# Convolution part of a two-layer image kernel: one more tap of the third channel block made by ScalarE and GpSimd, ScalarE's order around gelu changed

## The chip, the cores and the metric

The kernel runs on one core of one Trainium2 chip. The metric is the device time in microseconds (us) of one launch, the median of several runs. Short names: PE is TensorE's matmul, PEld its weight load, DVE is VectorE, ACT is ScalarE, POOL is GpSimd, SP is SyncE, which issues the DMAs.

## What is computed

Eight images of 384 channels and 64x64 pixels pass two layers. The first is a group norm and a linear attention with rotary embedding. The second, in which the change lies, is cut here to its body:

```python
t = jnp.einsum('bchw,oc->bohw', x, w_in)
tp = t.reshape(b, hid, hb, P, wb, P)
tf = jnp.fft.rfft2(tp, axes=(3, 5))
tf = tf * fft_filter[None, :, None, :, None, :]
tp = jnp.fft.irfft2(tf, s=(P, P), axes=(3, 5))
t = tp.reshape(b, hid, h, w)
t = jax.lax.conv_general_dilated(t, w_dw, window_strides=(1, 1), padding='SAME', feature_group_count=hid, dimension_numbers=('NCHW', 'OIHW', 'NCHW'))
x1, x2 = (t[:, :hid // 2], t[:, hid // 2:])
g = jax.nn.gelu(x1, approximate=False) * x2
return jnp.einsum('bchw,oc->bohw', g, w_out)
```

The layer's input is group-normed first and added to its result. P is 8: the transform works on patches of 8x8 pixels. The depthwise convolution has 3x3 = 9 taps for each channel.

## The kernel before

Images run one after the other, about 434.6 us each, in three parts: part A (queries, keys, values), part B (attention output, statistics) and the convolution part, `part_c` on each engine. An image is cut into NCH = 8 chunks of 8 pixel rows (512 pixels). The 384 channels are 3 blocks of 128, k = 0, 1, 2. All orders are written by hand: each engine has one fixed list of instructions, and they meet only at semaphores.

`part_c` runs steps c = 0 to 9 as a pipeline. In step c:

- PE makes four 128-pixel tiles of chunk c: `t_tile` (w_in, 9 matmuls), `dft_tile` (L1283), `inverse_tile` (L1290). It makes the first tap of blocks 0 and 1 of chunk c-1 (`taps`, L1317; all six first taps for the last chunk), and `out_block` 0, 1, 2 of chunk c-2 (L1302 to L1306, w_out). `out_block` waits for `s_rest`, which POOL's `gated_rest` raises, and for the residual additions of DVE that free its bank.
- ACT copies each tile out of its bank (`copy_t` L634, `copy_img` L640 into the padded image `filt_img`, which lies in `big`), computes gelu of chunk c-2 (`gelu`, L647 narrow and L649 wide), rounds the gated result (`round_gated`, L656 to L659), normalises a coming chunk (L557, L567), and makes products of chunk c-1: `product(c, q)` (L670) is tap q of block 2 times its weight, written into one of four slots of `prod`.
- POOL adds products 1 to 5 into slot 0 (`add_product`, L509), adds one block of a residual (`add_residual`, L516), takes the low parts of the gated result (`gated_rest`, L522 and L524), then adds product 5, and makes the low part of a coming chunk (`low_part`, L437).
- DVE makes the other taps (`tap(c, q, k)`, L1007), each one instruction that adds into PSUM. The first DVE tap of block 2 reads the sum in slot 0 of `prod` instead of the bank, so it waits for POOL's last addition. EARLY lists the taps of chunk c-1 done in step c, LATE those of chunk c-2. DVE also multiplies by the filter (`times_filter`, L987, four in a step), gates (L1015, L1022) and adds the output to the residual (`add_out`, L939).

Slot 0 is written anew by ACT's product 0 only after the DVE tap that reads it. ACT's gelu waits for taps (8, 2) and (8, 0). The first `taps` of PE waits for gelu wide, the second for the wide gate.

## Time and profile before

| | us |
|---|---|
| median of 3 runs (3548.68 to 3550.89) | 3549.17 |
| the profiled execution | 3545.66 |
| its span in the trace | 3543.9 |
| PE busy | 3318.6 |
| DVE busy | 2981.3 |
| POOL busy | 2042.9 |
| ACT busy | 1723.4 |

The difference of 1.8 us between the profiled time and the span lies around the program. Matmuls overlap each other in the trace, so the distance from one start to the next says more of PE than its busy time. The eight images repeat the same pattern; the rows below are all of the second image, whose convolution part runs from about 757 to 932 us, except the last of them, which is of the third.

### The profile page before, as it was taken

Reading aid. Unit: us, or ns where it says so; the run is one execution under the profiler, and the core shown is the slowest. Engines: PE = TensorE matmul, PEld = TensorE weight load, DVE = VectorE, ACT = ScalarE, POOL = GpSimd, SP = SyncE. Lnnn points to the kernel's source line nnn. Section 1 sums busy time; section 2 is a strip of 40 time slices with the busy share of each in tenths; the row PEclk is TensorE's granted clock in tenths of the full one; section 3 lists DMA queues with packets and bytes.
Section 4 is the critical chain, followed back from the end, with each engine's and each line's share of the span. In section 5 each row is a group of like instructions: output and inputs, shape, how many; then the busy total and the mean of one; then the engine's idle time right before and its main releaser. Section 6 shows DMA issues by size and latency. Waiting matters only on the chain. (4 is left out here: it accounts for less than half of the span.)

```text
span 3543.9 us, 50201 instructions
## 1 busy us (share of the span) xinstructions
PE 3318.6 (94%) x17374; PEld 2872.3 (81%) x17374; DVE 2981.3 (84%) x5231; ACT 1723.4 (49%) x3159; POOL 2042.9 (58%) x1343
## 2 busy tenths in 40 slices
PE   5999999999999999999999999998999999999998
PEld 4987779877797778977789777896779967799775
DVE  7877989779898798887989879888798887888887
ACT  2433854338443474435744257442664426644275
POOL 2555755547556475564755647456565565655665
PEclk9999999999999999999999999999999999999999
DMA  6215332143321432123332233213332133331422
GB/s 224 72 36 178 106 109 72 54 161 107 122 67 63 143 132 100 63 85 125 130 101 70 90 133 124 100 54 111 113 125 99 54 131 113 113 101 52 143 99 98
DMA packets 185341, 369.89 MB, mean 104 GB/s; under 512 B 7771, under 2 KB 8835, under 8 KB 184835
## 3 DMA queue, kind: packets, MB, share of 16 engines
q1 hardware_dynamic: 185090, 366.68, 30.3%
q8 instruction: 142, 2.33, 0.3%
q14 instruction: 109, 0.88, 0.1%
HBM read 265.99 MB, written 100.66 MB: 103 GB/s over the span
## 5 line engine op out<-in xcount | busy, mean ns | idle before, releaser
L1136 PE MATMUL bank<-w_hi,x_hi 128*128 128x384 f32 x2304 | 803.5, 349 | 17.9 <-ACT vt L578 10.7
L444 POOL TENSOR_TENSOR t<-t 128x768 f32<-128x768 f32 x256 | 535.3, 2091 | 466.4 <-DVE t L841 462.4
L1137 PE MATMUL bank<-w_lo,x_hi 128*128 128x384 f32 x2304 | 781.7, 339 | 0.0
L1007 DVE SCALAR_TENSOR_TENSOR bank<-big,wdw,bank 128x512 f32<-128x512 f32 x1072 | 749.1, 746 | 20.4 <-PE bank L1317 17.3
L437 POOL TENSOR_TENSOR x_lo<-xa,x_hi 128x512 fp32r<-128x512 f32 x360 | 459.4, 1292 | 478.4 <-ACT x_hi L567 478.4
L509 POOL TENSOR_TENSOR prod<-prod 128x512 f32<-128x512 f32 x320 | 410.5, 1283 | 244.5 <-ACT prod L670 224.9
L1141 PE MATMUL bank<-w_hi,x_lo 128*128 128x384 f32 x2304 | 533.1, 339 | 0.5 <-POOL x_lo L437 0.5
L572 ACT ACTIVATE t<-t 128x384 f32<-128x384 f32 x256 | 134.7, 526 | 759.5 <-POOL t L444 747.8
L1136 PEld LDWEIGHTS bank<-w_hi,x_hi 128*128 128x128 f32 x2304 | 436.8, 190 | 23.9 <-issue 22.7
L1137 PEld LDWEIGHTS bank<-w_lo,x_hi 128*128 128x128 f32 x2304 | 437.3, 190 | 1.1
L1141 PEld LDWEIGHTS bank<-w_hi,x_lo 128*128 128x128 f32 x2304 | 415.0, 189 | 1.4 <-POOL x_lo L437 1.4
L836 DVE TENSOR_TENSOR bank<-bank,qkbias 128x384 f32<-128x384 f32 x512 | 279.6, 559 | 137.9 <-PE bank L1141 137.6
L1136 PE MATMUL bank<-win_hi,x_hi 128*128 128x384 f32 x768 | 305.4, 398 | 0.9 <-ACT x_hi L567 0.4
L670 ACT ACTIVATE prod<-big,wdw 128x512 f32<-128x512 f32 x384 | 261.5, 715 | 71.5 <-DVE bank L1007 71.2
L1290 PEld LDWEIGHTS bank<-t_mats,gb 128*128 128x128 f32 x1536 | 205.4, 191 | 89.9 <-issue 35.5
L626 ACT ACTIVATE qt_hi<-bank 128x512 fp32r<-128x512 f32 x192 | 107.4, 594 | 314.8 <-PE bank L1217 314.8
L1137 PE MATMUL bank<-win_lo,x_hi 128*128 128x384 f32 x768 | 259.9, 338 | 0.0
L841 DVE TENSOR_TENSOR t<-bank,t_csw 128x384 f32<-128x384 f32 x512 | 258.4, 545 | 0.0
L1238 PE MATMUL bank<-qt_hi,mout_hi 128*128 128x512 f32 x576 | 247.7, 430 | 0.0
L1164 PE MATMUL bank<-vt,kt 128*128 128x129 f32 x1536 | 214.8, 275 | 25.6 <-DVE kt L853 25.6
L1290 PE MATMUL bank<-t_mats,gb 128*128 128x128 f32 x1536 | 217.1, 277 | 17.8 <-ACT big L640 9.4
L1164 PEld LDWEIGHTS bank<-vt,kt 128*128 128x128 f32 x1536 | 206.9, 190 | 30.6 <-DVE kt L853 30.6
(132 smaller groups left out, 6966.8 us busy)
## 6 DMA issues: line engine op xcount, KB each, us to landing
xr<-x SPq DMA_DIRECT2D x128, 768.0 KB, 4.7
xa<-x SPq DMA_DIRECT2D x64, 768.0 KB, 6.3
x_scratch<-xr SPq DMA_DIRECT2D x64, 768.0 KB, 3.3
xa<-x_scratch SPq DMA_DIRECT2D x64, 768.0 KB, 6.0
xr<-x_scratch SPq DMA_DIRECT2D x64, 768.0 KB, 4.8
out<-xr SPq DMA_DIRECT2D x64, 768.0 KB, 3.3
big<-x SPq DMA_DIRECT2D x8, 768.0 KB, 10.2
w_raw<-wqkv_t SPq DMA_DIRECT2D x1, 1728.0 KB, 6.8
```

What stands on the lines that cost most here:

```text
L437: nc.gpsimd.tensor_tensor(dst, src, hi, ALU.subtract).then_inc(s_lo, 1)
L444: nc.gpsimd.tensor_tensor(a, a, b[:, :, ::-1, :], ALU.add).then_inc(s_add, 1)
L509: nc.gpsimd.tensor_tensor(prod[:, 0], prod[:, 0], prod[:, slot_of(q)], ALU.add).then_inc(s_padd, 1)
L670: nc.scalar.activation(prod[:, slot_of(q)].rearrange("p (r s) -> p r s", s=W), filt_img[:, 2, ds(c * ROWS + q // 3, ROWS), q % 3:q % 3 + W ...
L836: nc.vector.tensor_tensor(qk, qk, qkbias[:, b * C:(b + 1) * C], ALU.add).then_inc(s_bias, 1)
L841: ins = nc.vector.tensor_tensor(dst[:, p2, b].rearrange("p s (f r) -> p s f r", r=2), src, tab.unsqueeze(1).unsqueeze(3).to_broadcast(wide ...
L1007: nc.vector.scalar_tensor_tensor(dst, src, wdw[:, k, q:q + 1], so_far, ALU.mult, ALU.add)\
L1136: nc.tensor.matmul(dst, hi(k), whi(k), start=(k == 0), stop=False)
L1137: nc.tensor.matmul(dst, hi(k), wlo(k), start=False, stop=False)
L1141: ins = nc.tensor.matmul(dst, lo(k), whi(k), start=False, stop=(k == KB - 1))
L1164: ins = nc.tensor.matmul(bank[KVB][:, k * (P + 1):(k + 1) * (P + 1)], kt[:, p2, k * P:(k + 1) * P], vt[:, p2, k, :], start=(first and k == ...
L1290: ins = nc.tensor.matmul(bank[INVB][:, k * P:(k + 1) * P], gb[:, p2, k * P:(k + 1) * P], phi_t, start=True, stop=True)
```

## The change

Tap 6 of block 2 is no longer a DVE instruction. ACT makes it as product 6 (slot 3) and POOL adds it, both at the start of the next step, ahead of their work for the next chunk. The first DVE tap of block 2 is then (7, 2). ACT's `copy_t` of tile 0 moves ahead of products 0 to 2. In step 2 alone those three products move behind gelu. In step 1 a one-element gelu is put ahead of the last `copy_img`, so that the table load stands there. The lists LATE and LAST have a new order.

```diff
-POOL_TAPS = 6
+POOL_TAPS = 7
-LATE = [(6, 2), (6, 0), (7, 2), (7, 0), (8, 2), (8, 0), (6, 1), (7, 1), (8, 1)]
+LATE = [(6, 0), (7, 0), (7, 2), (8, 0), (8, 2), (6, 1), (7, 1), (8, 1)]
-LAST = [(6, 2), (6, 0), (7, 2), (7, 0), (8, 2), (8, 0), (6, 1), (7, 1), (8, 1)]
+LAST = LATE
...
                 def part_c(c, h, edge, par):
+                    if c >= 2:
+                        add_product(c - 2, 6)
                     if within(edge, 0, NCH, -1):
                         for q in range(1, 3):
                             add_product(c - 1, q)
...
-                            act.wait_ge(s_dw, dw_count(i, c - 1, (6, 2)))
+                            act.wait_ge(s_dw, dw_count(i, c - 1, (7, 2)))
...
-                    if conv:
+                    if gated:
+                        if c < NCH + 1:
+                            act.wait_ge(s_img, (i * 8 + c - 1) * 4 + 6)
+                        product(c - 2, 6)
+                    if tile:
+                        copy_t(T, 0)
+                    if conv and c != 2:
                         for q in range(3):
                             product(c - 1, q, edge == 1)
-                    if tile:
-                        copy_t(T, 0)
...
                     if gated:
                         gelu(c - 2, edge == NCH + 1)
+                    if c == 2:
+                        for q in range(3):
+                            product(c - 1, q)
...
                         copy_img(T + 2, c, 2)
+                        if c == 1:
+                            nc.scalar.activation(idle_act[:, :], counted[:, 31:32], ACT.Gelu)
                         copy_img(T + 3, c, 3)
...
                     if last:
-                        for q, k in LAST[:6]:
+                        for q, k in LAST[:5]:
...
                         dve.wait_ge(s_img, T + 2)
-                        tap(c - 2, 6, 2)
                         tap(c - 2, 6, 0)
+                        tap(c - 2, 7, 0)
+                    if gated:
                         tap(c - 2, 7, 2)
-                    if gated:
-                        tap(c - 2, 7, 0)
+                        tap(c - 2, 8, 0)
                         tap(c - 2, 8, 2)
-                        tap(c - 2, 8, 0)
                         tap(c - 2, 6, 1)
```

ACT's list in step 2, from its first `prod` instruction to the one behind gelu's copy. Before (`prod` is a product, `tb` a `copy_t`, `gel` gelu):

```order
L670 ACTIVATE prod<-big,wdw 128x512 x3
L634 ACTIVATE tb<-bank0 128x384
L647 ACT_TABLE_LOAD
L647 ACTIVATE gel<-bank5 64x512
L649 ACTIVATE gel<-bank6 128x512
L634 ACTIVATE tb<-bank1 128x384
L670 ACTIVATE prod<-big,wdw 128x512
```

And now:

```order
L673 ACTIVATE prod<-big,wdw 128x512
L637 ACTIVATE tb<-bank0 128x384
L650 ACTIVATE gel<-bank5 64x512
L652 ACTIVATE gel<-bank6 128x512
L673 ACTIVATE prod<-big,wdw 128x512 x3
L637 ACTIVATE tb<-bank1 128x384
L673 ACTIVATE prod<-big,wdw 128x512
```

The three products stand behind gelu, and `copy_t` of tile 1 behind them. The single product ahead is tap 6 of chunk 0.

POOL's list in step 3 and every later step with tiles. Before (`prod` is `add_product`, `xr` the residual, `g_half` and `g_lo` are `gated_rest`):

```order
L509 TENSOR_TENSOR prod<-prod 128x512 x2
L516 TENSOR_TENSOR xr<-xr,vt 128x512
L509 TENSOR_TENSOR prod<-prod 128x512 x2
L522 TENSOR_TENSOR g_half<-gel,g_top 128x512
L524 TENSOR_TENSOR g_lo<-gel,g_hi 128x512
```

And now:

```order
L510 TENSOR_TENSOR prod<-prod 128x512 x3
L517 TENSOR_TENSOR xr<-xr,vt 128x512
L510 TENSOR_TENSOR prod<-prod 128x512 x2
L523 TENSOR_TENSOR g_half<-gel,g_top 128x512
L525 TENSOR_TENSOR g_lo<-gel,g_hi 128x512
```

One addition, that of product 6 of chunk c-2, stands ahead of the rest.

DVE's list at the start of a steady step. Before (bank5 is the sum of block 2, bank6 of block 0, bank7 of block 1):

```order
L1007 SCALAR_TENSOR_TENSOR bank5<-big,wdw,prod 128x512
L1007 SCALAR_TENSOR_TENSOR bank6<-big,wdw,bank6 128x512
L1007 SCALAR_TENSOR_TENSOR bank5<-big,wdw,bank5 128x512
L1007 SCALAR_TENSOR_TENSOR bank6<-big,wdw,bank6 128x512
L1007 SCALAR_TENSOR_TENSOR bank5<-big,wdw,bank5 128x512
L1007 SCALAR_TENSOR_TENSOR bank6<-big,wdw,bank6 128x512
L1007 SCALAR_TENSOR_TENSOR bank7<-big,wdw,bank7 128x512
```

And now:

```order
L1019 SCALAR_TENSOR_TENSOR bank6<-big,wdw,bank6 128x512 x2
L1019 SCALAR_TENSOR_TENSOR bank5<-big,wdw,prod 128x512
L1019 SCALAR_TENSOR_TENSOR bank6<-big,wdw,bank6 128x512
L1019 SCALAR_TENSOR_TENSOR bank5<-big,wdw,bank5 128x512
L1019 SCALAR_TENSOR_TENSOR bank7<-big,wdw,bank7 128x512
```

One tap is gone, and the tap that reads `prod` is the third instead of the first.

## Rows read from the trace of the kernel before

**Rows 1.** Stretch, busy PE, PEld, DVE, ACT, POOL, clock, DMA share, GB/s: step 4

```profile
826.93:844.99 18.06, 17.66 (x88) 14.18 (x87) 17.45 (x28) 14.45 (x26) 13.73 (x11) 1.00 0.37 132
```

**Rows 2.** Timeline, PE, step 4: start, busy, operation [idle before <-releaser]

```profile
826.93 0.34 PE L1136 MATMUL bank<-win_hi,x_hi 128*128 128x384 f32 x1
...
827.98 0.68 PE L1141 MATMUL bank<-win_hi,x_lo 128*128 128x384 f32 x3
...
830.07 0.81 PE L1283 MATMUL bank<-tb,t_mats 128*128 128x384 f32 x2
...
837.13 0.81 PE L1283 MATMUL bank<-tb,t_mats 128*128 128x384 f32 x2
...
838.36 0.47 PE L1302 MATMUL bank<-g_hi,wout_hi 128*128 128x512 f32 x1
...
839.60 0.81 PE L1283 MATMUL bank<-tb,t_mats 128*128 128x384 f32 x2
...
841.42 0.47 PE L1302 MATMUL bank<-g_hi,wout_hi 128*128 128x512 f32 x1
...
844.99 0.34 PE L1136 MATMUL bank<-win_hi,x_hi 128*128 128x384 f32 x1
```

**Rows 3.** Timeline of DVE, same step

```profile
826.13 1.05 DVE L1007 SCALAR_TENSOR_TENSOR bank<-big,wdw,prod 128x512 f32<-128x512 f32 x1
...
831.04 0.55 DVE L987 TENSOR_TENSOR gb<-bank,fsel 128x384 f32<-128x384 f32 x1
...
840.60 0.68 DVE L939 TENSOR_TENSOR xr<-bank,xr 128x512 f32<-128x512 f32 x1
...
842.92 0.69 DVE L939 TENSOR_TENSOR xr<-bank,xr 128x512 f32<-128x512 f32 x1 [0.52 <-PE bank L1306]
```

**Rows 4.** Timeline of ACT, same step

```profile
827.27 1.96 ACT L670 ACTIVATE prod<-big,wdw 128x512 f32<-128x512 f32 x3 [1.30 <-DVE bank L1007]
...
829.13 0.47 ACT L634 ACTIVATE tb<-bank 128x384 f32<-128x384 f32 x1
...
843.52 0.51 ACT L640 ACTIVATE big<-bank 128x384 f32<-128x384 f32 x1 [1.24 <-PE bank L1290]
```

**Rows 5.** Timeline of POOL, same step

```profile
828.70 2.72 POOL L509 TENSOR_TENSOR prod<-prod 128x512 f32<-128x512 f32 x2 [2.07 <-ACT prod L670]
...
831.37 1.19 POOL L516 TENSOR_TENSOR xr<-xr,vt 128x512 f32<-128x512 f32 x1
...
836.41 1.28 POOL L524 TENSOR_TENSOR g_lo<-gel,g_hi 128x512 fp32r<-128x512 f32 x1
```

**Rows 6.** Timeline of ACT, POOL and PE, step 2 of the same image

```profile
795.60 0.60 ACT L649 ACTIVATE gel<-bank 128x512 f32<-128x512 f32 x1
...
801.17 1.27 POOL L524 TENSOR_TENSOR g_lo<-gel,g_hi 128x512 fp32r<-128x512 f32 x1
...
802.50 0.50 PE L1302 MATMUL bank<-g_hi,wout_hi 128*128 128x512 f32 x1
...
805.23 0.47 PE L1302 MATMUL bank<-g_hi,wout_hi 128*128 128x512 f32 x1
```

**Rows 7.** Timeline of DVE, steps 8 and 9 of the same image

```profile
899.04 1.34 DVE L1007 SCALAR_TENSOR_TENSOR bank<-big,wdw,prod 128x512 f32<-128x512 f32 x1 [0.59 <-ACT big L640]
...
912.11 0.76 DVE L1007 SCALAR_TENSOR_TENSOR bank<-big,wdw,prod 128x512 f32<-128x512 f32 x1 [4.75 <-POOL prod L509]
...
916.28 0.69 DVE L1015 TENSOR_TENSOR gel<-gel,bank 64x512 f32<-64x512 f32 x1
...
919.99 1.28 DVE L939 TENSOR_TENSOR xr<-bank,xr 128x512 f32<-128x512 f32 x2
```

**Rows 8.** Timeline of PE, behind two long idle times

```profile
920.82 0.69 PE L1302 MATMUL bank<-g_hi,wout_hi 128*128 128x512 f32 x1 [3.52 <-DVE xr L939]
...
1103.13 0.94 PE L1164 MATMUL bank<-vt,kt 128*128 128x129 f32 x6 [2.02 <-DVE kt L853]
...
1103.82 1.18 PE L1113 MATMUL bank<-w_hi,win_hi 128*128 128x512 f32 x4
```

More of the change, by code:

```diff
@@ L168, in build_program @@
         counted = sb("counted", [P, 32])
+        idle_act = sb("idle_act", [P, 1])
         ksum = sb("ksum", [P, KB])
@@ L535, in part_c @@
                     if within(edge, 0, NCH, -1):
-                        for q in range(3, POOL_TAPS - 1):
+                        for q in range(3, 5):
                             add_product(c - 1, q)
@@ L540, in part_c @@
                     if within(edge, 0, NCH, -1):
-                        add_product(c - 1, POOL_TAPS - 1)
+                        add_product(c - 1, 5)
                     if c != 1 and c < (NCH if i + 1 < images else NCH - 1):
@@ L1044, in part_c @@
                     if last:
-                        for q, k in LAST[:6]:
+                        for q, k in LAST[:5]:
                             tap(c - 2, q, k, last)
                         gate_narrow(c - 2, last)
-                        for q, k in LAST[6:]:
+                        for q, k in LAST[5:]:
                             tap(c - 2, q, k, last)
```

## Prediction

> **What bounds the kernel now.** I read the table of busy times by stretch first, then the timelines of the four engines over one step of the second image's convolution part. A full step takes 18.06 us; DVE is busy for 17.45 of it, PE for 17.66, ACT for 14.45, POOL for 13.73 [rows 1]. The reader is to see there that two engines are nearly full and that ACT and POOL seem to have room for one more operation each.
>
> The timelines tell more: the engines hang in loops. PE starts its step at 826.93 and the next at 844.99 [rows 2]. DVE waits in the step once, 0.52 us at 842.92, for PE's output block 1 [rows 3]; that block starts at 841.42, behind DVE's addition of 840.60 plus 0.68 [rows 2, 3]. POOL waits 2.07 us for the first product and works from 828.70 without a gap to the end of `g_lo` at 836.41 + 1.28 = 837.69 [rows 5]. PE's output block 0, which needs `g_lo`, starts at 838.36 [rows 2], 0.67 later. So the chain from ACT's first product over POOL to PE has a slack of 0.67 us at most in 18. The question of this change is when those products start.
>
> **DVE's part of the change.** One tap out of eight behind the first goes: (831.04 - 826.13 - 0.96) / 6 = 0.66 us from start to start, the first taking 0.96 of its 1.05 [rows 3]. Taps (6, 0) and (7, 0) now follow each other, and the second waits for the first; in step 9 two gates of 0.69 and three taps of one block in a row take 919.99 - 916.28 = 3.71 us [rows 7], (3.71 - 1.38) / 3 = 0.78 for each such tap, so 0.12 is lost again. The bare gain is about 0.54 us a step. What is late next: `times_filter` of tile 0 stands behind these taps and needs PE's `dft_tile`, which starts at 830.07, and DVE takes it up at 831.04 [rows 2, 3], 0.97 later. The matmul pair itself lasts 0.81, so of the 0.54 at most 0.97 - 0.81 = 0.16 can be used before DVE waits there for PE. That loop (PE's start of a step, `dft_tile`, DVE's step, output block 1, PE's next step) allows 17.9 us a step and no less.
>
> **When the products start now.** Before, they start at 827.27, right behind the end of the first DVE tap at 827.18 [rows 3, 4]: 0.34 us after PE's step begins. Now two things stand ahead of them.
>
> Loop 1, over `copy_t`. It waits for PE's tile 0, whose last matmuls end at 827.98 + 0.68, 1.73 us into PE's step [rows 2]; hand-over 0.05; the copy's 0.47 less the overlap of 0.10 (829.13 follows 827.27 by 1.86, while the three products last 1.96) is 0.37 [rows 4]. From the products to the end of `g_lo` it is 837.69 - 827.27 = 10.42, with nothing new inside (product 6's addition is done before) [rows 4, 5]. Then PE's output block 0 follows within 0.06, as in step 2 (801.17 + 1.27 = 802.44, then 802.50) [rows 6]. Block 0 to block 1 is 839.60 - 838.36 = 1.24, and a `dft_tile` with its `inverse_tile` 838.36 - 837.13 = 1.23 [rows 2]: 2.47, where it was 3.06. Block 1 to PE's next step is 844.99 - 841.42 = 3.57 [rows 2]. Sum 1.73 + 0.05 + 0.37 + 10.42 + 0.06 + 2.47 + 3.57 = 18.67 us.
>
> Loop 2, over product 6. Output block 1 to the last image copy 843.52 - 841.42 = 2.10, the copy 0.51 and 0.07 to be seen [rows 2, 4]; product 6 (1.96 + 2 x 0.10) / 3 = 0.72 [rows 4] and 0.08; POOL's addition 1.30 (half of 2.72 is 1.36 [rows 5]) and 0.05; so tap (7, 2) starts 4.83 behind block 1. It takes 0.76 with POOL idle, as at 912.11 [rows 7], then 0.09 to the products, 10.48 to output block 0, 2.47 to block 1. Sum 18.63.
>
> Both are longer than 18.06, and nearly equal. A steady step becomes 18.67: +0.61. There are four full steps (3 to 6): +2.4 us an image. DVE's saved time turns into a wait for POOL at tap (7, 2) of about half a microsecond.
>
> At tap (7, 2) the profile shows two prices: 1.05 us at 826.13 while POOL works on `low_part`, 0.76 at 912.11, where POOL had just ended [rows 3, 7]. I take 0.76, since POOL now has nothing to do until the products that wait for this tap; with 1.05 loop 2 is 18.93 and the time 8 us more, which the range holds. The Trainium skill (SBUF — State Buffer, Who interferes with whom) says that a DVE instruction with two SBUF inputs and a GpSimd instruction that reads SBUF shut each other out, and that others don't. By it this is the short tap, and the sum stays; were it the long one everywhere, as in most steps of before, the 8 us come on top. The two durations agree with it.
>
> **Step 2.** Here the products follow gelu. Gelu wide starts at 795.60 [rows 6]; the table load ahead of it is gone, but so is the early start of DVE's taps (copy, product 6, addition and tap (7, 2) come first), so I leave it there, give or take 0.2. The products then start at 796.1, and `g_lo` ends 10.42 later, less the residual that this step lacks (1.19, of which 0.05 overlaps [rows 5]): 805.4. Before it was 802.44. Output block 1 follows at 805.4 + 0.06 + 2.47 = 807.9 instead of 805.23 [rows 6]: +2.6 us (2.3 to 2.8). The table load moved to step 1 costs ACT some tenths before the last image copy, and is hidden by the same chain.
>
> **Steps 7 to 9.** In step 7 ACT carries one product more before it reaches the late image copies: 0 to 0.8, I take 0.4. In step 8 the chain runs over DVE's tap of 899.04, which waited 0.59 for ACT's image copy and ended at 900.38 [rows 7], 1.36 behind that copy. Now it is 0.07 + 0.72 + 0.08 + 1.30 + 0.05 + 0.76 = 2.98: +1.6. POOL's chain to the last addition is as long as before, plus one addition: +1.3. DVE waits for that chain (4.75 us at 912.11 [rows 7]). After it, DVE took 919.99 - 912.11 = 7.88 us to the output addition on which PE waits 3.52 us [rows 7, 8]. Now (6, 0) and (7, 0) are done before the wait; (7, 2), (8, 0), (8, 2) take 2.1, gelu narrow 0.8, and the rest the same 3.71: 6.6, so -1.3. Together +1.6 (0.8 to 2.2).
>
> **The sum.** 2.6 + 2.4 + 0.4 + 1.6 = 7.0 us an image, 56 us for eight. The profiled execution becomes 3545.66 + 56 = 3601.7; it stands 3.5 below the median, so the median becomes 3605.
>
> **Rivals.**
>
> *DVE is the bound and its time comes back.* Price: 0.54 us in six steps of eight images, 26 us, 3523; with the loop over `dft_tile` in force only 0.16, 8 us, 3541. For it: DVE is the fullest engine beside PE, and its single wait is short [rows 1, 3]. Against it: it needs the products no later than before, and the code puts a copy and an addition ahead of them. The Trainium skill (Perfetto Trace Analysis, Optimizing Scalar/DVE Operations) holds that with DVE saturated, handing work to Scalar or even GpSimd may make sense, and (Identifying the Most-Contended Engine) to optimize the engine of highest occupancy first. By that rule the sum would be this rival's; the slack of 0.67 behind POOL is what the busy shares don't show.
>
> *The steady steps keep their time.* If the products start within 0.67 us of where they started, only step 2 and the tail cost: (2.6 + 1.6) x 8 = 34, 3583. It decides at the start of the products behind PE's step: under 1.0 us it is this, at my 2.15 it is the forecast.
>
> *PE also loses its clock.* In step 2 PE would sit idle about 2 us for `g_lo` and 1 us for a copy. After 3.52 us of idle time its matmul took 0.69 instead of 0.47 [rows 2, 8]; ten of these are 2 us an image, 16 in all: 3621. Against it: behind 2.02 us of idle time four matmuls of 512 columns last 1.18 us in all [rows 8], the pace of output block 0's five in 1.24 [rows 2].
>
> **How the numbers follow.** Forecast 0.65 (3595 to 3615), steady steps unharmed 0.12 (3583), clock loss 0.10 (3621), DVE's time comes back 0.10 (3523 to 3544), no change 0.03. The range 3577 to 3632 leaves out the last two and a little at either end: the step-2 and tail bounds are 0.3 + 0.8 down and 0.2 + 0.6 up an image, 9 and 6 us, the long tap 8. 0.2% is 7 us, about what can be told from no change: faster 0.10, same 0.03, slower 0.87.
>
> **What would show it.** In the new trace: DVE waits for POOL at the tap that reads `prod` in steps 3 to 7; the products start about 2.1 us behind PE's step; POOL's `g_lo` ends right before PE's output block 0, and PE waits for it; steps of 18.7 us; in step 2 the block starts near 805.4 on the old scale. Wrong would be a PE without that wait, or steps of 18.0 us or less.

## The result, and the profile after

| | before | after |
|---|---|---|
| median, us | 3550.03 (4 runs, 3548.68 to 3552.57) | 3614.92 (4 runs, 3612.78 to 3617.21) |
| profiled span, us | 3543.9 | 3613.4 |
| mean granted clock | 0.98 | 0.979 |

The change costs 65 us: ratio 1.0182, 95% interval 1.0164 to 1.0200. The forecast was +56, 3605; the range 3577 to 3632 holds the time.

The page of the changed kernel, first its busy times (engine, busy us, share of the span, number of instructions), then groups of its table of costs (line, engine, operation, count | busy us, mean ns of one | idle time just before them and what ended most of it):

```profile
PE 3324.6 (92%) x17374; PEld 2882.3 (80%) x17374; DVE 2953.3 (82%) x5167; ACT 1767.0 (49%) x3231; POOL 2122.4 (59%) x1407
...
L1019 DVE SCALAR_TENSOR_TENSOR bank<-big,wdw,bank 128x512 f32<-128x512 f32 x1008 | 720.4, 750 | 65.0 <-PE bank L1328 54.4
...
L510 POOL TENSOR_TENSOR prod<-prod 128x512 f32<-128x512 f32 x384 | 494.4, 1287 | 298.7 <-ACT prod L673 276.3
```

DVE has 64 instructions and 28 us less than before, as intended: 8 taps in each of 8 images, at 0.44 us net. ACT and POOL have 44 and 80 us more. PE has the same instructions and stands still longer. These shares look better than before, and the kernel is slower; where the time went is read from the waits. The next rows are of the same place as before, a steady step of the second image (start, busy, operation, and in brackets the idle time before it with what ended it). DVE, ACT, POOL and PE of the changed kernel, one fence each:

```profile
839.23 0.76 DVE L1019 SCALAR_TENSOR_TENSOR bank<-big,wdw,prod 128x512 f32<-128x512 f32 x1 [0.47 <-POOL prod L510]
...
849.54 0.56 DVE L999 TENSOR_TENSOR gb<-bank,fsel 128x384 f32<-128x384 f32 x1 [0.16 <-PE bank L1294]
...
854.68 0.69 DVE L951 TENSOR_TENSOR xr<-bank,xr 128x512 f32<-128x512 f32 x1 [0.66 <-PE bank L1317]
```

```profile
837.10 0.72 ACT L673 ACTIVATE prod<-big,wdw 128x512 f32<-128x512 f32 x1
839.81 0.49 ACT L637 ACTIVATE tb<-bank 128x384 f32<-128x384 f32 x1 [1.99 <-PE bank L1152]
840.19 1.94 ACT L673 ACTIVATE prod<-big,wdw 128x512 f32<-128x512 f32 x3
```

```profile
837.90 1.30 POOL L510 TENSOR_TENSOR prod<-prod 128x512 f32<-128x512 f32 x1 [0.40 <-ACT prod L673]
841.60 2.72 POOL L510 TENSOR_TENSOR prod<-prod 128x512 f32<-128x512 f32 x2 [2.40 <-ACT prod L673]
...
849.33 1.30 POOL L525 TENSOR_TENSOR g_lo<-gel,g_hi 128x512 fp32r<-128x512 f32 x1
```

```profile
831.94 0.50 PE L1313 MATMUL bank<-g_hi,wout_hi 128*128 128x512 f32 x1 [0.50 <-POOL g_lo L525]
834.45 0.48 PE L1313 MATMUL bank<-g_hi,wout_hi 128*128 128x512 f32 x1
...
844.00 1.10 PE L1328 MATMUL bank<-big,tapdiag 128*128 128x512 f32 x2 [0.43 <-ACT gel L652]
850.67 0.50 PE L1313 MATMUL bank<-g_hi,wout_hi 128*128 128x512 f32 x1 [0.51 <-POOL g_lo L525]
853.17 0.48 PE L1313 MATMUL bank<-g_hi,wout_hi 128*128 128x512 f32 x1
```

Output block 0 comes every 850.67 - 831.94 = 18.73 us where it was 18.06 [rows 1, 2]. POOL had been waited for by nobody in this step; now PE waits 0.50 us for its `g_lo`. The products start at 840.19, behind a `copy_t` that waits 1.99 us for PE's tile 0. DVE's gain has become waits: 0.47 for POOL, 0.16 and 0.66 (before 0.52 [rows 3]) for PE.

Step 2 of the same image, ACT and then PE:

```profile
796.40 1.28 ACT L734 ACT_TABLE_LOAD   x1
...
802.63 0.59 ACT L650 ACTIVATE gel<-bank 64x512 f32<-64x512 f32 x1 [2.95 <-DVE bank L1019]
...
803.74 1.93 ACT L673 ACTIVATE prod<-big,wdw 128x512 f32<-128x512 f32 x3
```

```profile
803.99 1.10 PE L1328 MATMUL bank<-big,tapdiag 128*128 128x512 f32 x2 [1.03 <-ACT gel L652]
806.10 0.91 PE L1294 MATMUL bank<-tb,t_mats 128*128 128x384 f32 x2 [1.02 <-ACT tb L637]
813.21 0.50 PE L1313 MATMUL bank<-g_hi,wout_hi 128*128 128x512 f32 x1 [1.77 <-POOL g_lo L525]
```

PE waits three times, 3.82 us in all, behind an ACT that sits idle for 2.95 us. DVE's tap (7, 2), on which product 0 waits, ends at 801.22, so for the last 1.4 us of that time ACT could have made products.

To compare runs I count from one mark, ACT's root of the group norm's variance, which opens the convolution part (757.55 us in the second image before, 765.50 after). Between it and the table load for exp that follows the part, before took 171.0 us on average over the seven images that have one, after 179.0: 8.0 an image, 64 in eight. The change's cost lies here. The rest of an image, whose code is the same in all kernels of this document, takes 263.6 us on average in the profile of before, 264.3 in that of after and 264.2 to 265.1 in those of the experiments.

### The profile page after: what moved, and what is told of

It reads as the page before. It is cut to its first block and busy times, and to the rows that moved or that the text cites. A ratio compares the mean times of both kernels' runs of the same rounds, so it can differ in the third digit from the quotient of the medians.

```text
span 3613.4 us, 50449 instructions
## 1 busy us (share of the span) xinstructions
PE 3324.6 (92%) x17374; PEld 2882.3 (80%) x17374; DVE 2953.3 (82%) x5167; ACT 1767.0 (49%) x3231; POOL 2122.4 (59%) x1407
## 5 line engine op out<-in xcount | busy, mean ns | idle before, releaser
L1019 DVE SCALAR_TENSOR_TENSOR bank<-big,wdw,bank 128x512 f32<-128x512 f32 x1008 | 720.4, 750 | 65.0 <-PE bank L1328 54.4
L510 POOL TENSOR_TENSOR prod<-prod 128x512 f32<-128x512 f32 x384 | 494.4, 1287 | 298.7 <-ACT prod L673 276.3
L673 ACT ACTIVATE prod<-big,wdw 128x512 f32<-128x512 f32 x448 | 306.4, 716 | 19.9 <-DVE bank L1019 18.0
L1328 PE MATMUL bank<-big,tapdiag 128*128 128x512 f32 x416 | 205.2, 609 | 41.1 <-ACT gel L652 41.1
L999 DVE TENSOR_TENSOR gb<-bank,fsel 128x384 f32<-128x384 f32 x256 | 141.8, 554 | 115.2 <-PE bank L1294 93.6
```

Source lines behind the costliest of these rows:

```text
L510: nc.gpsimd.tensor_tensor(prod[:, 0], prod[:, 0], prod[:, slot_of(q)], ALU.add).then_inc(s_padd, 1)
L673: nc.scalar.activation(prod[:, slot_of(q)].rearrange("p (r s) -> p r s", s=W), filt_img[:, 2, ds(c * ROWS + q // 3, ROWS), q % 3:q % 3 + W ...
L1019: nc.vector.scalar_tensor_tensor(dst, src, wdw[:, k, q:q + 1], so_far, ALU.mult, ALU.add)\
```

## The experiments

"Before" is always the kernel before, timed together with that row's kernel on the same chip. "Behind the mark" is the distance from that root in the second image.

| kernel | median, us | before, us | ratio (95%) | steady step |
|---|---|---|---|---|
| the change | 3614.9 | 3550.0 | 1.0182 (1.0164 to 1.0200) | 18.73 |
| step 2 undone | 3591.5 | 3544.5 | 1.0126 (1.0108 to 1.0143) | 18.71 |
| products first | 3641.4 | 3544.5 | 1.0264 (1.0247 to 1.0281) | 19.36 |
| gated rest first | 3641.0 | 3544.5 | 1.0265 (1.0245 to 1.0286) | 19.54 |
| two sums | 3621.1 | 3544.5 | 1.0209 (1.0191 to 1.0227) | 18.72 |
| addition 6 small | 3593.3 | 3547.4 | 1.0123 (1.0110 to 1.0137) | 18.71 |
| residual small | 3592.6 | 3547.4 | 1.0123 (1.0107 to 1.0138) | 18.34 |
| gelu's load alone | 3553.5 | 3549.8 | 1.0010 (1.0001 to 1.0019) | 18.07 |
| two sums, products first | 3607.0 | 3549.8 | 1.0161 (1.0147 to 1.0175) | 18.83 |
| the same, POOL holds | 3565.3 | 3547.4 | 1.0042 (1.0029 to 1.0054) | 17.95 |
| the same, repaired | 3539.0 | 3548.4 | 0.9975 (0.9966 to 0.9984) | 17.98 |
| before, sum sooner | 3536.3 | 3548.4 | 0.9968 (0.9955 to 0.9980) | 18.06 |
| repaired, hold in the tail | 3544.1 | 3549.7 | 0.9982 (0.9973 to 0.9991) | 17.97 |

The steady step is output block 0 to output block 0, the mean of the four from step 3 to step 7; before it was 18.06.

### Step 2 undone

```diff
-                    if conv and c != 2:
+                    if conv:
                         for q in range(3):
                             product(c - 1, q, edge == 1)
...
-                    if c == 2:
-                        for q in range(3):
-                            product(c - 1, q)
```

> The changed kernel with one part undone: in step 2 the products 0 to 2 stand ahead of gelu again, as in all other steps. Theory (the chain from ACT's products over POOL's additions and gated_rest to PE's output block 0 sets the time): in the changed kernel the products of step 2 start at 803.74, behind gelu; ahead of it they can start right behind tap (7, 2), which ends at 801.22, so about 2.4 us sooner; output block 0 comes 2.4 sooner (PE itself would be ready about then), 19 us in all for eight images: 3596 us. Rival (gelu and the first taps of PE, which wait for it, are what step 2 hangs on): gelu comes 0.5 us or more later than now, so the kernel gets slower by 4 us or more, 3619.

Measured 3591.5. Output block 0 of step 2 comes 45.33 us behind the mark, where it came 47.71 after the change and 44.95 before. PE of this kernel:

```profile
805.92 1.10 PE L1325 MATMUL bank<-big,tapdiag 128*128 128x512 f32 x2 [1.70 <-ACT gel L652]
812.09 0.50 PE L1310 MATMUL bank<-g_hi,wout_hi 128*128 128x512 f32 x1
```

The wait for `g_lo` is gone and the one for gelu is longer, 1.70 instead of 1.03. By the ratios 0.0056 of 3550, 20 us, a third of the whole cost, is the special order of step 2. That order alone served gelu and delayed everything POOL does. With it undone block 0 of step 2 comes only 0.4 us later than before the change, so nearly all that is lost in this step comes from the order and not from the seventh tap.

### Two other orders of the same work

Products ahead of `copy_t` again, as before:

```diff
-                    if tile:
-                        copy_t(T, 0)
                     if conv and c != 2:
                         for q in range(3):
                             product(c - 1, q, edge == 1)
+                    if tile:
+                        copy_t(T, 0)
```

> The changed kernel with ACT's products 0 to 2 ahead of the first copy_t again, as before the change (step 2 as changed). Theory: the products gain nothing, because tap (7, 2), on which product 0 waits, ends at 839.99 and they start at 840.19 now; but the copy then stands behind them and reaches PE's first dft_tile 1.2 us late, and with it times_filter and all of DVE's step. Steady step 19.3 us instead of 18.73, five steps: 3633 to 3640 us. Rival (the copy alone delays the products): faster, steady step near 18.1, 3590.

Measured 3641.4 over a kernel before of 3544.5, so 97 us, 1 us over the expected range; the step of 19.3 came as expected. ACT and PE of a steady step:

```profile
844.79 0.72 ACT L673 ACTIVATE prod<-big,wdw 128x512 f32<-128x512 f32 x1
847.77 1.95 ACT L673 ACTIVATE prod<-big,wdw 128x512 f32<-128x512 f32 x3 [2.26 <-DVE bank L1019]
849.63 0.47 ACT L637 ACTIVATE tb<-bank 128x384 f32<-128x384 f32 x1
```

```profile
850.16 0.91 PE L1294 MATMUL bank<-tb,t_mats 128*128 128x384 f32 x2 [1.13 <-ACT tb L637]
```

Loop 2 is closed over `copy_t` here: product 6, addition 6, tap (7, 2), products, and only then the copy, for which PE waits 1.13 us. The step is 19.36. So the change's move of `copy_t` is a repair that its seventh tap needs; it holds the loss in a steady step to 0.67 us where it would be 1.3.

`gated_rest` ahead of additions 3 and 4 in steps 2 to 7, so that `g_lo` comes sooner:

```diff
+                    if 2 <= c < NCH:
+                        gated_rest(c - 2)
                     if within(edge, 0, NCH, -1):
                         for q in range(3, 5):
                             add_product(c - 1, q)
-                    if c >= 2:
+                    if c >= NCH:
                         gated_rest(c - 2)
```

> The changed kernel with POOL's gated_rest moved ahead of its additions of products 3 and 4 in steps 2 to 7. Theory (PE waits for g_lo behind POOL's additions): in a steady step g_half can start when the rounding is done, 6.95 us behind the first product, and g_lo ends at about 9.56 instead of 10.45; output block 0 no longer waits, and the next loop (gelu wide, PE's first taps, the third dft_tile, times_filter, output addition) sets the step at 18.3 to 18.4 instead of 18.73; in step 2 output block 0 comes 1.6 us sooner. Per image 1.6 + 5 x 0.36 = 3.4, 27 us in all: 3588 us. Rival (tap (7, 2) and product 6 hold the step, whatever POOL's order): no change, 3615. Rival (DVE lost its time to PE through gelu alone): no change in the steady step.

Measured 3641.0: wrong, and by much. POOL, DVE and PE:

```profile
830.21 1.30 POOL L523 TENSOR_TENSOR g_half<-gel,g_top 128x512 fp32r<-128x512 f32 x1 [1.75 <-ACT gel L662]
...
832.71 4.14 POOL L510 TENSOR_TENSOR prod<-prod 128x512 f32<-128x512 f32 x3
836.81 3.78 POOL L438 TENSOR_TENSOR x_lo<-xa,x_hi 128x512 fp32r<-128x512 f32 x3
840.54 1.29 POOL L510 TENSOR_TENSOR prod<-prod 128x512 f32<-128x512 f32 x1
```

```profile
841.87 0.76 DVE L1021 SCALAR_TENSOR_TENSOR bank<-big,wdw,prod 128x512 f32<-128x512 f32 x1 [1.75 <-POOL prod L510]
```

```profile
846.53 1.10 PE L1330 MATMUL bank<-big,tapdiag 128*128 128x512 f32 x2 [1.60 <-ACT gel L654]
```

PE no longer waits for `g_lo`. But POOL now idles 1.75 us for the rounded gate, pays for it behind, and from 830.21 to 841.83 has no gap; addition 6 comes late, DVE's tap waits 1.75 for it, and gelu with PE behind it 1.60. POOL looked 59% busy over the span, yet in this order it has no room between one wait that is built in (tap to products) and the next.

### Which loop sets the step

The two loops of the prediction were 18.67 and 18.63, too near to each other for the step's length to tell them apart. Addition 6 stands in loop 2 alone:

```diff
-                    nc.gpsimd.tensor_tensor(prod[:, 0], prod[:, 0], prod[:, slot_of(q)], ALU.add).then_inc(s_padd, 1)
+                    w = 1 if q == 6 else CHUNK
+                    nc.gpsimd.tensor_tensor(prod[:, 0, :w], prod[:, 0, :w], prod[:, slot_of(q), :w], ALU.add).then_inc(s_padd, 1)
```

> The change, with POOL's seventh-tap addition cut to one column of 512 (the rest of that tap's product is left out of the result). It takes about 1.2 us out of the loop over product 6, that addition and the tap (forecast 18.63), and nothing between PE's tile 0 and g_lo (forecast 18.67). Theory A (the loop through copy_t(T,0), the products, POOL and g_lo sets the steady step): the step stays at 18.7 us; only steps 2, 8 and 9, where the addition stands on the path, get 1.2 us shorter at two or three places: 3590 to 3606 us. Rival B (POOL's total work sets the step): the step falls by 0.6 to 0.7, the whole by 2.4 per image more: 3565 to 3585 us.

Measured 3593.3, and the steady step is unchanged. POOL and PE:

```profile
836.23 0.19 POOL L511 TENSOR_TENSOR prod<-prod 128x1 f32<-128x1 f32 x1 [0.37 <-ACT prod L674]
839.94 2.72 POOL L511 TENSOR_TENSOR prod<-prod 128x512 f32<-128x512 f32 x2 [3.52 <-ACT prod L674]
```

```profile
830.28 0.50 PE L1314 MATMUL bank<-g_hi,wout_hi 128*128 128x512 f32 x1 [0.49 <-POOL g_lo L526]
...
849.00 0.50 PE L1314 MATMUL bank<-g_hi,wout_hi 128*128 128x512 f32 x1 [0.48 <-POOL g_lo L526]
```

849.00 - 830.28 = 18.72. POOL is given 1.1 us of room in each step and uses it to wait longer, 3.52 instead of 2.40. The 21 us that the kernel gains come from step 2 (0.7 us an image) and the tail. Part of the tail's gain, 0.9 us an image, lies behind PE's long wait there, where the granted clock stayed higher, and not in the addition itself. So loop 1, and not loop 2, sets the steady step.

The residual addition stands in both loops:

```diff
-                    nc.gpsimd.tensor_tensor(mine, mine, proj_c, ALU.add).then_inc(s_res, 1)
+                    nc.gpsimd.tensor_tensor(mine[:, :1, :1], mine[:, :1, :1], proj_c[:, :1, :1], ALU.add).then_inc(s_res, 1)
```

> The change, with POOL's residual addition cut to one element (the rest of that residual is left out of the result). The addition stands in both loops, so both get about 1.1 us shorter, to 17.5 us, under the 18.06 us that PE's work takes. Theory A: the steady step is 18.0 to 18.1 us again, the output block waits for PE's own order and not for g_lo, and the whole is 3590 to 3602 us (four or five steps of 0.65 us and up to 0.9 us in steps 3 to 7's neighbours, times 8 images). Rival B (the step is set by something that doesn't run through POOL): the step stays at 18.7 us and the whole within 4 us of the change, 3611 to 3619 us.

Measured 3592.6, inside what was expected, but not by the step that was expected: 18.34, not 18.0 to 18.1. ACT and PE:

```profile
836.93 0.49 ACT L637 ACTIVATE tb<-bank 128x384 f32<-128x384 f32 x1 [1.95 <-PE bank L1152]
837.32 1.94 ACT L673 ACTIVATE prod<-big,wdw 128x512 f32<-128x512 f32 x3
...
839.76 0.59 ACT L650 ACTIVATE gel<-bank 64x512 f32<-64x512 f32 x1
```

```profile
841.12 1.10 PE L1328 MATMUL bank<-big,tapdiag 128*128 128x512 f32 x2 [0.42 <-ACT gel L652]
```

The wait for `g_lo` is gone and a third loop remains, which the prediction didn't have: PE's tile 0, `copy_t`, the products and both gelus, which now run one behind the other on ACT without a gap, and PE's taps, which wait 0.42. From the copy to PE's taps it is 841.12 - 836.93 = 4.19, in the changed kernel too (844.00 - 839.81). From the taps to output block 0, to block 1 and to the next copy it is 6.16, 2.65 and 5.34 in this kernel's rows: with the 4.19 together 18.34, the step. In the changed kernel this loop is hidden under loop 1.

### Two sums

The change starts the sum of a chunk in slot 0 and must wait with product 0 until DVE has read the last one. With a sum for even and one for odd chunks that wait goes:

```diff
-                    nc.gpsimd.tensor_tensor(prod[:, 0], prod[:, 0], prod[:, slot_of(q)], ALU.add).then_inc(s_padd, 1)
+                    nc.gpsimd.tensor_tensor(prod[:, c % 2], prod[:, c % 2], prod[:, slot_of(c, q)], ALU.add).then_inc(s_padd, 1)
...
-                            act.wait_ge(s_dw, dw_count(i, c - 1, (7, 2)))
+                        if c >= 2:
+                            act.wait_ge(s_dw, dw_count(i, c - 2, (7, 2)))
```

> The changed kernel with two slots for the sum of the products, used in turn by even and odd chunks (the other products share the two remaining slots), so that product 0 no longer waits for tap (7, 2) of the chunk before; ACT's order as changed. Theory (two loops of equal length hold the products: tap (7, 2), and the first copy_t, which waits for PE's tile 0): freeing one of the two moves nothing, 3612 to 3616 us, steady step 18.7. Rival (the added hop ACT, POOL, DVE of product 6 alone is the cause): the products start at once and the step falls to 18.1, 3585 or less. Seen by now: with both holds taken away the kernel took 3607, so a time near 3615 or a little over is likelier than 3585.

Measured 3621.1, a little over what was expected; the two ratios' intervals overlap. The steady step is 18.72 as with one sum, as loop 1 says: that order never waited for the slot. The convolution part takes 179.2 us behind the mark, the change's 179.0: it loses 1.8 us in step 2 (49.54 for block 0), where only two slots are left for the other products, and gets nearly all of it back in the tail, 1.0 us by a granted clock that stayed higher behind PE's long wait.

Two sums and the products first, without the order of step 2:

```diff
                     if conv:
                         for q in range(3):
                             product(c - 1, q, edge == 1)
+                    if tile:
+                        copy_t(T, 0)
```

> The changed kernel with both holds on the products taken away at once: two slots for the sum in turn (product 0 doesn't wait for tap (7, 2) of the chunk before) and products 0 to 2 ahead of the first copy_t, in step 2 too. All the work is that of the changed kernel: seven products on ACT, six additions on POOL, eight other taps less one on DVE. Theory (it is when the products start, not how much work ACT and POOL have): the products start about 0.3 us ahead of PE's step, g_lo is early again, and the loop over PE's first dft_tile and DVE holds the step at 17.9 us; the last steps save 0.7 us. About 1.4 us an image under the kernel before: 3538 us. Rival (the added product and addition, 0.7 and 1.3 us a step, are themselves too much): 3600 or more. Rival (product 6's hop still delays DVE at tap (7, 2) and gelu with it): between the two, 3560.

Measured 3607.0, far from 3538 and in the range of the rival by which the added work is too much in itself. DVE and POOL:

```profile
838.71 1.78 DVE L1016 SCALAR_TENSOR_TENSOR bank<-big,wdw,prod 128x512 f32<-128x512 f32 x1 [0.48 <-POOL prod L510]
```

```profile
837.37 4.25 POOL L510 TENSOR_TENSOR prod<-prod 128x512 f32<-128x512 f32 x3 [0.16 <-ACT prod L673]
```

The tap that reads `prod` takes 1.78 us where it took 0.76. POOL no longer stops for it: the first of the three additions makes the sum that the tap reads, the second starts with the tap. Gelu then waits 1.60 us for DVE (in this kernel's ACT timeline), and the step is 18.83. So the wait that I had taken away was also what kept the two engines apart. If that is so, it must help to put a wait in:

```diff
                     if within(edge, 0, NCH, -1):
+                        if c >= 2:
+                            gp.wait_ge(s_dw, dw_count(i, c - 2, (7, 2)))
                         for q in range(1, 3):
                             add_product(c - 1, q)
```

> The kernel of two sums with the products first, with one more wait: POOL begins the next chunk's additions only when DVE's tap (7,2), which reads the other sum from SBUF, is done; the one-element gelu is left out. Theory A (in the run before this one that tap took 1.77 us instead of 0.76 because POOL's additions ran beside it, and gelu, the gates and PE waited for that microsecond): the tap is back at about 0.76 us, DVE gives the gelu its bank 1.0 us sooner, POOL's additions start 1.1 us later, which the 1.64 us that POOL waits ahead of the low parts takes up; the steady step goes from 18.83 to 18.0 to 18.2 us and the whole to 3540, between 3532 and 3552 us, as fast as the kernel before or a little faster. Rival B (the tap's length is its own, two operands from SBUF): it stays at 1.77 us, the additions only come later, and the whole is 3610 to 3640 us. Rival C (the tap is short, but POOL's chain of additions, residual and g_lo is then the last to arrive at the output block): step 18.4 to 18.8, the whole 3565 to 3605 us.

The one-element gelu of step 1 is left out too; alone it costs some 4 us, below. Measured 3565.3; by the ratios 42 us less, nearly all by one added wait, with the added product and addition still there. So they are not what made 3607. DVE, POOL and ACT:

```profile
850.13 0.76 DVE L1015 SCALAR_TENSOR_TENSOR bank<-big,wdw,prod 128x512 f32<-128x512 f32 x1 [0.47 <-POOL prod L509]
```

```profile
850.97 2.73 POOL L509 TENSOR_TENSOR prod<-prod 128x512 f32<-128x512 f32 x2 [0.87 <-DVE bank L1015]
```

```profile
788.82 0.72 ACT L674 ACTIVATE prod<-big,wdw 128x512 f32<-128x512 f32 x1 [2.05 <-POOL prod L509]
...
798.02 1.28 ACT L651 ACT_TABLE_LOAD   x1 [1.06 <-DVE bank L1015]
```

The tap is 0.76 again and the step 17.95, 0.1 shorter than before the change. That is the mechanism shown, from both sides. The 14 traces of this case hold 896 such taps: 675 ran with POOL idle and took 0.75 or 0.76 us each; 221 began while a POOL instruction was under way and took 0.84 to 1.78, and every one of these ended 0.55 to 0.56 us after that instruction did, whichever it was. POOL pays too: in the kernel of 3607 the addition that begins during the tap takes 1.53 to 1.56 us instead of 1.29.

The Trainium skill (SBUF — State Buffer, Who interferes with whom) states it: a DVE instruction with two SBUF inputs contends for a shared read interface with a GpSimd instruction that reads SBUF, the lock is exclusive, and the order of issue decides who is blocked. The traces agree with it. By that rule an addition of 1.29 us that has just begun and then the tap's own 0.76 would make about 2.0, an estimate; 1.78 is what stands here, because only 0.56 of the tap is left when POOL ends.

The total missed, 3565 instead of 3540. That is the edge of rival C's range, but the longer step by which C gets there (18.4 to 18.8) is not there. The last two rows are of steps 1 and 2: with two sums only two slots are left for the other products, so ACT waits 2.05 us in step 1, and the table load stands behind a wait of 1.06 us for DVE. Output block 0 of step 2 is 46.78 behind the mark, not 44.95.

### Gelu's table sooner, alone

The kernel before with the one-element gelu of the change in step 1:

```diff
                        copy_img(T + 2, c, 2)
+                        if c == 1:
+                            nc.scalar.activation(idle_act[:, :], counted[:, 31:32], ACT.Gelu)
```

> The kernel before with one part of the change alone: the one-element gelu in step 1, so that the table load stands there. Theory: in step 2 of before gelu narrow starts at 794.98 behind a load of 1.28; without the load gelu, product 3 and g_lo come about 1.2 us sooner, and output block 0 of step 2 with them, less 0.3 us for the image copy that the load now delays: 0.6 to 1.1 us an image, 3541 to 3545 us. Rival (the load was hidden by PE or DVE): no change, 3550.

Measured 3553.5 to 3549.8: no gain, rather 0.1% lost. DVE and ACT in step 2:

```profile
792.11 0.76 DVE L1010 SCALAR_TENSOR_TENSOR bank<-big,wdw,prod 128x512 f32<-128x512 f32 x1 [0.31 <-ACT big L641]
```

```profile
795.60 0.59 ACT L648 ACTIVATE gel<-bank 64x512 f32<-64x512 f32 x1 [0.31 <-DVE bank L1010]
```

The load delays the image copy behind it; DVE starts step 2 0.31 us late, and gelu, rid of its load, waits 0.31 for DVE. Output block 0 stands 44.85 behind the mark instead of 44.95, and the whole part takes 171.5 instead of 171.0; 0.3 of that lies behind PE's long wait of the tail, where the granted clock differs from image to image.

### A version that beats both, and its control

Three repairs on the kernel in which POOL holds: three slots for the products of chunk 0 (whose other sum is not yet in use), the table load into the 1.06 us in which ACT waits in step 2, and, in the last product step, additions 5 and 6 ahead of `gated_rest`:

```diff
-            return c % 2 if q == 0 else 3 - q % 2
+            if q == 0:
+                return c % 2
+            return 1 + (q - 1) % 3 if c == 0 else 3 - q % 2
...
+                    if c == 2:
+                        nc.scalar.activation(idle_act[:, :], counted[:, 31:32], ACT.Gelu)
                     if 3 <= c <= NCH:
...
+                    if c == NCH:
+                        for q in range(5, 7):
+                            add_product(c - 1, q)
                     if c >= 2:
                         gated_rest(c - 2)
```

> The kernel of two sums in which POOL holds its additions for the tap, with three repairs where its trace still shows time lost against the kernel before. (1) The first chunk of an image has three slots for its products instead of two: ACT's fifth product waited 2.05 us for a slot in step 1, with copy_t behind it, and the last picture copy of that step came 1.0 us late. (2) gelu's table is loaded in step 2 behind copy_t(T,0), in the 1.06 us in which ACT waits for DVE, by a one-element gelu there. (3) In the last product step POOL adds products 5 and 6 ahead of the gated rest: the last chunk's tap (7,2) waited 1.96 us for that sum, and the output block of that step had 3.7 us to spare. Theory A: steps 2 to 7 are then 0.3 us shorter than the kernel before's over all, the tail loses 1.3 to 2.0 us of its 35.34 us from the output block of step 7 to the last one (34.65 in the kernel before); in all 1.0 to 2.0 us per image faster than the kernel before: 3532 to 3541 us at 3547 us for that one. Rival B: step 2 is held by POOL (product 6, then the wait for the tap, then four additions and the rest), the repairs 1 and 2 give half, and only the tail is better: 3540 to 3552 us.

Measured 3539.0 (11 runs, 3535.0 to 3542.7): 0.25% under the kernel before. Output block 0 of step 2 is back at 44.97 behind the mark and that of step 7 at 134.69 (before 135.00, with POOL holding 136.04). From there to the first output block of the last chunk it takes 32.57 us, where it took 34.65 and 35.34. That is 2.8 less, over the 1.3 to 2.0 expected: half of it is DVE's earlier chain, half a faster PE (5.36 us instead of 6.86 for the stretch behind its long wait). That half was not planned: on average over seven images the part ends 7.4 us behind that wait instead of 8.3, because the granted clock stayed higher, some 7 us in eight images. The last section comes back to it.

The third repair has nothing to do with the seventh tap, so the kernel before got it too, with its one late addition:

```diff
+                    if c == NCH:
+                        add_product(c - 1, POOL_TAPS - 1)
                     if c >= 2:
                         gated_rest(c - 2)
```

> The kernel before with one change: in the last product step POOL adds product 5 ahead of the gated rest and not behind it. Control for repair 3 of the run beside it: how much of its gain has to do with the seventh tap. In the kernel before DVE's tap (6,2) of the last chunk waits 4.75 us for that sum, until 912.11 us; the sum would be there 2.55 us sooner, and g_lo 1.3 us later, at 912.2, where the output block starts at 914.5. Theory A: DVE's last chain starts 2.2 to 2.5 us sooner and takes add_out and the last output block with it: 3527 to 3533 us at 3547 us for the kernel before. Rival B: the last chain then waits for PE's taps of the last chunk instead, and 0 to 1 us per image is left: 3539 to 3547 us.

Measured 3536.3 (5 runs, 3532.4 to 3540.5), between the two theories. DVE of this kernel, last step:

```profile
909.12 1.75 DVE L1009 SCALAR_TENSOR_TENSOR bank<-big,wdw,prod 128x512 f32<-128x512 f32 x1 [2.65 <-POOL prod L509]
```

Before, that wait was 4.75 [rows 7]. The tap starts 2.1 us sooner, but now beside POOL's `g_half`, and takes 1.75 instead of 0.76. So 1.1 us are gained there, and the part takes 169.8 us behind the mark instead of 171.0. The intervals of this kernel and the repaired one overlap: six products for block 2 with this one line are as good as seven with all repairs. In the two traces the repaired kernel reaches the end of PE's long wait 0.3 us sooner in an image, 2 us in eight, which the times don't resolve. The whole idea of a seventh tap is worth nothing that I can measure, even carried out well.

The last run held POOL in the tail too:

```diff
                         for q in range(5, 7):
                             add_product(c - 1, q)
+                        gp.wait_ge(s_dw, dw_count(i, c - 1, (7, 2), True))
```

> The repaired kernel with POOL holding its additions for the tap once more: in the last product step the gated rest begins only when DVE's tap (7,2) of the last chunk is done. In the repaired kernel that tap took 1.54 us (910.17) beside POOL's additions and g_half (909.89); alone such a tap took 0.76 us. Theory A (the length comes from POOL's operation beside it): the tap is 0.76 us again, DVE's last chain of the image is 0.7 to 0.8 us shorter, g_half starts 0.7 us later, for which the output block has 0.4 us; 0.4 to 0.8 us per image less: 3532 to 3537 us at 3548.4 us for the kernel before. Rival B (the tap waits for something else there, PE's taps or the clock): it stays at 1.5 us and the whole at 3538 to 3542 us.

Measured 3544.1: a miss; it gains nothing, and by the ratios is rather 2 us behind (their intervals overlap). DVE and ACT of this kernel, then ACT's same row of the repaired one:

```profile
910.17 0.76 DVE L1029 SCALAR_TENSOR_TENSOR bank<-big,wdw,prod 128x512 f32<-128x512 f32 x1
```

```profile
913.54 0.59 ACT L658 ACTIVATE gel<-bank 64x512 f32<-64x512 f32 x1 [5.67 <-POOL g_lo L527]
```

```profile
913.12 0.59 ACT L657 ACTIVATE gel<-bank 64x512 f32<-64x512 f32 x1 [5.26 <-DVE bank L1028]
```

The tap is 0.76 and not 1.54, as theory A had it. But I had looked for `g_lo`'s slack only at the output block. Gelu writes into the buffer that `g_lo` reads, so the held `g_lo` holds gelu, 0.42 us later than without, and everything behind it.

## Why the prediction was right, step by step

**The direction and the mechanism** were right: the slack of POOL's chain behind PE, not DVE's busy share, decides. The rival by which DVE's time comes back fell in this order of the code. The Trainium skill (Perfetto Trace Analysis, Optimizing Scalar/DVE Operations) says that with DVE saturated, handing work to Scalar or even GpSimd may make sense. Here it didn't: DVE had 28 us less to do and the kernel took 65 us more.

**Loop 1**, forecast 18.67, is 18.73 from output block 0 to the next. Its terms in the rows of after: output block 1 to the copy 839.81 - 834.45 = 5.36 (forecast 3.57 + 1.73 + 0.05 = 5.35), copy to products 0.38 (0.37), products to the end of `g_lo` 850.63 - 840.19 = 10.44 (10.42), to block 0 0.04 (0.06), block 0 to 1 2.50 (2.47). Each is off by 0.03 at most. That it is this loop and not loop 2 the small addition 6 has shown.

**Loop 2**, forecast 18.63, was not the bound. The price of 0.76 for the tap was right, and for the reason given: POOL idles there.

**DVE's gain.** The wait of 0.47 for POOL at the tap was forecast as about half a microsecond, and DVE waits for PE ahead of `times_filter` (0.16).

**Step 2**, forecast +2.6 at output block 1 (its terms, 805.4 + 0.06 + 2.47 against 805.23, make 2.7): against the mark it is 50.21 instead of 47.68, +2.53. Gelu wide came 0.3 us sooner than where the forecast left it, and the way from the products to block 0 is 0.1 longer. Undone, it gave back 20 us, 2.5 an image.

**Steady steps 3 to 6**, forecast +2.4: block 1 of step 2 to block 1 of step 6 is 74.92 against 72.31, +2.61.

**Step 7**, forecast +0.4: block 1 of step 6 to block 2 of step 7 is 21.13 against 20.67, +0.46. **Steps 8 and 9**, forecast +1.6 up to the output addition on which PE waits: +1.64. Two rows of DVE there:

```profile
928.62 0.76 DVE L1019 SCALAR_TENSOR_TENSOR bank<-big,wdw,prod 128x512 f32<-128x512 f32 x1 [2.25 <-POOL prod L510]
...
935.18 1.28 DVE L951 TENSOR_TENSOR xr<-bank,xr 128x512 f32<-128x512 f32 x2
```

The three parts hold one by one: POOL's first addition of step 8 comes 1.55 us later behind block 2 of step 7 (forecast 1.6), from it to this tap it is 1.41 longer (1.3), and from the tap to the output addition 935.18 - 928.62 = 6.56 instead of 7.88 (6.6). Together 7.2 an image against 7.0.

**What was short** is for the most part a term that wasn't there: PE's clock behind its long wait of the tail. From the output block that ends this wait to the end of the part it is 7.75 us before and 8.22 after, on average over seven images. PE in the tail, of before in [rows 8] and of after here, then the table by stretch (stretch, then PE, PEld, DVE, ACT, POOL busy with counts, granted clock, DMA share, GB/s), one stretch of after and then one of before:

```profile
936.01 0.76 PE L1313 MATMUL bank<-g_hi,wout_hi 128*128 128x512 f32 x1 [3.77 <-DVE xr L951]
```

```profile
940.00:942.00 2.00, 2.00 (x8) 2.00 (x7) 2.00 (x5) 0.44 (x1) 2.00 (x2) 0.53 0.86 331
```

```profile
923.00:925.00 2.00, 2.00 (x10) 1.99 (x8) 1.68 (x4) 1.71 (x3) 0.40 (x1) 0.67 0.00 0
```

Before, the clock was at half behind the wait of 3.52 us [rows 8] and back some 3.5 us after its end (0.67 in this stretch, then 1.00). After, behind 3.77 us, it is at half from 936 to 938 and on to nearly 942. The part ends 8.2 and 8.3 us behind that block in these two images, so they differ little; the others make the difference. Where the clock stays at 1.00 or falls late it is 7.2 or 7.3, as in three images of before (the first, fifth and sixth) and in none of after, which has 7.8 once and 8.3 six times. The rival had PE lose its clock in step 2, in every image; it did so once in eight, in the third image, behind the wait of 1.80 us at 1257.84, where block 0 to block 1 took 3.46 us instead of 2.50. So the clock did cost about 3 us in the tail and 1 to 2 us in step 2: it was the right suspect at the wrong place.

The sum, by image: up to PE's long wait 7.2 more in five images, 7.5 in the first and 9.1 in the third, 53 in seven; 0.5 behind the wait in each of the seven, 3; and 8.5 in the last image, up to its last output block. That is 64.5, and the medians differ by 65. Why the first image has 0.3 more and the last 1.2 more than the 7.2 is not shown.

**What the prediction didn't see** is the third loop of 18.34 over gelu, and that PE waits 0.43 us in it already. It changes no number, but any repair of loop 1 ends there, as the small residual did.

## What to carry to other kernels

An engine at 59% can have no room: where the engines hand one sum round in loops, cost an added instruction at the loop that it stands in, with every buffer that its result holds, and not at the busy shares. When a wait is taken away, ask what it kept apart; POOL and a DVE instruction with two SBUF inputs were faster with a wait between them, some 40 us for one line. And test a rearrangement on the old kernel as well: the part that brought the gain here had nothing to do with the change.

## What was unexpected in the hardware

- The tap that reads `prod` and `big`, both in SBUF, has several durations for the same 128x512 work: 0.76 us with POOL idle (839.23), 1.05 to 1.34 us in places of the kernel before [rows 3, 7], up to 1.78 us with a POOL instruction that started just ahead. One rule gives them all: it ends 0.56 us after the POOL instruction that was under way at its start. The taps that read PSUM and `big` take 0.66 us from start to start beside the same POOL work. The Trainium skill's section above names this pair.
- The low clock behind PE's long wait of the tail doesn't follow the length of that wait. In one execution of the repaired kernel the wait is 2.19 to 2.24 us in each of the first seven images. Up to the first output block of the last chunk PE then took 5.36 us in three of them, with a granted clock of 1.00 throughout, 5.93 in three more and 6.45 in one, with the clock at half for a part of it. Behind 2.93 us (small residual, second image) it stayed at 1.00 too; behind 2.65 (hold in the tail) it was at 0.53 from 920 to 922, and behind 3.77 (the change) at half for nearly six us, 7.08 us in all. On average the part ends 7.2 to 8.0 us behind the wait in the kernels in which it is 2.2 to 2.9 us, and 7.7 to 8.3 in those in which it is 3.2 to 3.8. What decides a single image these runs don't settle. Up to 1.1 us of an image's length hangs on it, so a difference of a few us between two kernels can be this alone.
